# A graph network on one core: place registers loaded four at a time, restored columns queued behind x, widths built last, layer-one steps ahead of the drain

## What is computed

```python
h = relu(layernorm(x))
for W_r, W_sl, W_el in two_layers:
    agg = segment_sum((rel_embed[type] + h[src]) @ W_r, dst)
    h = rrelu(agg * deg ** -0.5 + where(deg == 0, h @ W_el, h @ W_sl))
x = x + h
h = relu(layernorm(x))
qk = h @ Wqk + bqk
scores = clip(sum(qk[dst] * qk[src]) / sqrt(128), -5, 5)
attn = segment_softmax(scores, dst)
x = x + layernorm(segment_sum(attn * v[src], dst) @ Wo + bo + h) * gamma + beta
```

## Time and profile before

| | before |
| --- | --- |
| median of 3 runs | 843.01 us (837.35 to 843.52) |
| the profiled execution | 839.33 us, span 836.7 us |
| mean granted TensorE clock | 0.973 |
| busy: PE, DVE, ACT, POOL | 722.0, 516.0, 431.7, 248.3 us |
| bytes moved by DMA | 27.89 MB, mean 33 GB/s |

### The profile page before, as it was taken

The page is one execution under the profiler, slowest core; times in us unless marked ns, Lnnn a source line. Parts: engine busy times, 40 slices in busy tenths (PEclk is TensorE's granted clock), DMA queues, the critical chain, the costliest instruction groups (busy, mean ns, idle before and its releaser), DMA issues.

```text
span 836.7 us, 15353 instructions
## 1 busy us (share of the span) xinstructions
PE 722.0 (86%) x5767; PEld 537.5 (64%) x5767; DVE 516.0 (62%) x931; ACT 431.7 (52%) x1085; POOL 248.3 (30%) x273
## 2 busy tenths in 40 slices
PE   4355787897879898988998899979999999999995
PEld 2245676797868788878887799834444444444455
DVE  4887997887767777724232333434475666565667
ACT  0435864555645555554211111257677676767672
POOL 7040020001001021110000000046666666666663
PEclk9999979999999999999999999999999999999997
DMA  4100200032310000010222211120000000000010
GB/s 127 41 1 16 60 5 8 2 94 75 98 46 8 8 8 7 7 63 3 66 65 87 63 38 38 38 97 15 1 13 12 13 13 11 15 3 23 1 26 18
DMA packets 39763, 27.89 MB, mean 33 GB/s; under 512 B 5311, under 2 KB 38163, under 8 KB 39686
## 3 DMA queue, kind: packets, MB, share of 16 engines
q1 hardware_dynamic: 38356, 26.02, 10.8%
q10 hardware_dynamic: 1330, 0.86, 0.4%
HBM read 13.28 MB, written 10.80 MB: 29 GB/s over the span
## 4 chain that ended last, share of the span: by engine, by line
PE 60%; DMA 10%; DVE 9%; issue 8%; ACT 7%; SPq 3%; ACTq 2%; POOL 1%; POOLq 0%; DVEq 0%
PE sums L1465 15%; PE sums L1448 15%; PE sums L997 9%; PE sums L1070 6%; PE sums L1036 6%; DMA work<-in_x 4%; DMA first_columns<-counts 2%; ACT counts L1238 2%; DMA h_attention<-work 2%; SPq L572 2%; DVE work L834 2%; DVE work L828 2%; ACTq L1214 1%; PE sums L1017 1%; PE sums L1004 1%
## 5 line engine op out<-in xcount | busy, mean ns | idle before, releaser
L1544 POOL TENSOR_TENSOR counts<-counts,work 125x500 f32<-125x500 f32 x150 | 165.5, 1104 | 96.6 <-DVE work L1605 89.5
L1036 PE MATMUL sums<-work 125*128 125x196 f16 (+15 forms) x1220 | 155.6, 255 | 24.6 <-DVE work L834 24.5
L1605 DVE SCALAR_TENSOR_TENSOR work<-sums,counts 125x500 f32<-125x500 f32 x150 | 101.7, 678 | 108.0 <-ACT sums L1562 108.0
L1465 PE MATMUL sums<-work 125*128 125x500 f32 (+1 forms) x350 | 158.6, 543 | 8.0 <-DVE work L1609 3.3
L828 DVE TENSOR_TENSOR work<-work,counts 125x3024 f16<-125x3024 f16 (+1 forms) x60 | 114.3, 1906 | 62.4 <-PE sums L1038 59.2
L1448 PE MATMUL sums<-work 128*125 128x500 f32 x300 | 150.3, 583 | 0.6 <-ACT work L1299 0.6
L1557 ACT ACTIVATE sums<-sums,work 125x500 f32<-125x500 f32 (+1 forms) x157 | 102.1, 650 | 76.3 <-PE sums L1448 73.0
L1238 ACT CAST counts<-sums 128x364 f32 (+38 forms) x305 | 132.1, 473 | 2.1 <-issue 1.4
L1038 PE MATMUL sums<-work 125*128 125x10 f16 (+15 forms) x800 | 132.5, 195 | 0.0
L997 PE MATMUL sums<-counts 125*128 125x250 f16 (+1 forms) x975 | 119.6, 267 | 9.5 <-ACT work L1180 9.5
L834 DVE TENSOR_TENSOR work<-work,counts 125x4200 f16<-125x4200 f16 (+15 forms) x120 | 125.5, 1087 | 0.0
(11 more groups left out here) (177 smaller groups left out, 660.9 us busy)
## 6 DMA issues: line engine op xcount, KB each, us to landing
first_columns<-counts SPq DMA_DIRECT2D x5, 610.4 KB
counts<-first_columns SPq DMA_DIRECT2D x5, 610.4 KB
counts<-counts SPq DMA_DIRECT2D x5, 468.8 KB
counts<-in_x SPq DMA_DIRECT2D x5, 312.5 KB
h_nodes<-counts SPq DMA_DIRECT2D x5, 312.5 KB
work<-in_x SPq DMA_DIRECT2D x12, 125.0 KB
x_after_messages<-work SPq DMA_DIRECT2D x12, 125.0 KB
h_attention<-work SPq DMA_DIRECT2D x12, 125.0 KB
```

Of the source, the lines that this page charges most:

```text
L1036: pe.matmul(win[:, 0:c, cols], lo[:, k * 2 * LO:k * 2 * LO + 128], m[:, k, h0 * w:(h0 + c) * w].rearrange("p (h d) -> p h d", d=w), start= ...
L1465: last = pe.matmul(ps_o[c % 2][:, 0:cols(u) // n], h3[:, j + i, :], pbuf[u % PB][:, i * NP:i * NP + cols(u) // n], start=j + i == 0, stop= ...
L1544: pool.tensor_tensor(a, a, p, ALU.add).then_inc(acc_done, 1)
L1605: dve.scalar_tensor_tensor(pbuf[u % PB], ps_s[u % 4][0:NP, 0:WIDE], float(np.exp(-CLIP)), counts[0:NP, j, c * WIDE:(c + 1) * WIDE], ALU.ma ...
```

## The change

Four edits. ScalarE loads the place registers four at a time (`CHUNK = 4`), so 50 loads of 4 take the place of 10 loads of 20. SyncE queues the restore of the columns directly behind the x load of its chunk instead of behind the h3 store. GpSimd builds `w_c` behind the identity matrix and signals `tables_done` a first time before it (with the memset of `power`) and a second time after it (with the memset of `one`), and VectorE waits for the second ahead of the first use of `w_c`. ScalarE's own, self and rest steps stand between the carry copy and the drain of their group.

```diff
@@ -607,13 +607,13 @@
                     sp.wait_ge(L["h3_out"], 16 * i)
                     sp.wait_ge(L["h3_turned"], i)
                 sp.dma_start(xc, by_block(x, c)).then_inc(L["x_in"], 16)
+                if i < 5:
+                    v = slice(5 * i, 5 * i + 5)
+                    sp.dma_start(counts[0:NP, v, 0:HEAD], heads.rearrange("p (j d) -> p j d", d=HEAD)[:, v, :]).then_inc(heads_in, 16)
                 sp.wait_ge(L["x2_ready"], i + 1)
                 sp.dma_start(by_block(x2, c), tmp).then_inc(L["x2_out"], 16)
                 sp.wait_ge(L["h3_ready"], i + 1)
                 sp.dma_start(h3[:, c * LB * D:(c + 1) * LB * D], xc.rearrange("p b f -> p (b f)")).then_inc(L["h3_out"], 16)
-                if i < 5:
-                    v = slice(5 * i, 5 * i + 5)
-                    sp.dma_start(counts[0:NP, v, 0:HEAD], heads.rearrange("p (j d) -> p j d", d=HEAD)[:, v, :]).then_inc(heads_in, 16)
             sp.wait_ge(L["summed"], CHUNKS)
             sp.wait_ge(L["h3_out"], 16 * LAST)
             for i, (j0, j1) in enumerate(T["h3_pieces"]):
@@ -651,18 +651,18 @@
             link(pool.tensor_scalar(starts, starts, 0.0, None, ALU.max))
             by_group(limit, [(0, float(KEY_AT - SPANS[1])), (KEY_GROUP, float(PART_AT - SPANS[1])), (PART_GROUP, float(N + PAD - SPANS[1]))])
             by_group(room, [(0, float(SPANS[0] - 1)), (ONE_BANK, float(SPANS[1] - 1))])
-            widths = [(first_group(b), float(w)) for b, (_, w) in enumerate(BATCHES) if b == 0 or w != BATCHES[b - 1][1]]
-            by_group(w_c, widths)
             pool.memset(power, -0.5).then_inc(tables_done, 1)
-            pool.iota(iota_f, pattern=[[1, NB * WM + WM % 2]], base=0, channel_multiplier=0).then_inc(iota_done, 1)
             pool.memset(ident_h[:, :], 0.0).then_inc(consts, 1)
             pool.wait_ge(consts, 1)
             pool.affine_select(out=ident_h[:, :], in_=ident_h[:, :], compare_op=ALU.not_equal, fill=1.0, base=0,
                                pattern=[[-1, 128]], channel_multiplier=1).then_inc(consts, 1)
+            widths = [(first_group(b), float(w)) for b, (_, w) in enumerate(BATCHES) if b == 0 or w != BATCHES[b - 1][1]]
+            by_group(w_c, widths)
+            pool.memset(one, 1.0).then_inc(tables_done, 1)
+            pool.iota(iota_f, pattern=[[1, NB * WM + WM % 2]], base=0, channel_multiplier=0).then_inc(iota_done, 1)
             by_group(least, [(0, 0.0)] + [(READY[c], float(LB * NP * (c + 1))) for c in range(CHUNKS - 1)])
             pool.memset(carry[:, 0, :], 0.0).then_inc(carry_ready, 1)
             pool.memset(ones_h, 1.0).then_inc(outside_set, 1)
-            pool.memset(one, 1.0).then_inc(outside_set, 1)
             pool.memset(T["outside"][:, :], 0.0).then_inc(outside_set, 1)
             pool.wait_ge(tables_done, 1)
             pool.wait_ge(stats_done, NB)
@@ -726,6 +726,7 @@
             link(dve.tensor_scalar(t_f, src_i, float(-(NP // 2)), 1.0 / NP, ALU.add, ALU.mult))
             link(dve.tensor_scalar(hi, t_f, ROUND, -ROUND, ALU.add, ALU.add))
             dve.scalar_tensor_tensor(key16[0], hi, float(-NP), src_i, ALU.mult, ALU.add).then_inc(nat_done, 1)
+            dve.wait_ge(tables_done, 2)
             for h in range(2):
                 last = dve.scalar_tensor_tensor(halves(key16[1], h), halves(hi, h), w_c[:, h:h + 1], halves(loc, h), ALU.mult, ALU.add)
             last.then_inc(nat_done, 1)
@@ -755,7 +756,7 @@
                 link(dve.tensor_tensor(by_tile(bad[:, 2:2 + RT]), by_tile(nx), over(w_c), ALU.is_ge))
                 link(dve.tensor_tensor(bad[:, 2 + RT:2 + 2 * RT], base, tb, ALU.is_lt))
                 link(dve.tensor_tensor(bad[:, at + 1:at + 3], by_tile(base)[:, :, 0], limit, ALU.is_gt))
-                dve.wait_ge(outside_set, 3)
+                dve.wait_ge(outside_set, 2)
                 link(dve.tensor_tensor(bad[:, at + 3:at + 5], by_tile(base)[:, :, 0], least, ALU.is_lt))
                 link(dve.memset(bad[:, at + 5:], 0.0))
                 link(dve.tensor_scalar(bad[0:1, at + 5:], base[0:1, 0:1], 0.0, None, ALU.is_gt))
@@ -974,7 +975,7 @@
                     if c:
                         pe.wait_ge(agg_out, c if c <= DIRECT else DIRECT + 1 if c == LAST else DIRECT)
                     else:
-                        pe.wait_ge(outside_set, 3)
+                        pe.wait_ge(outside_set, 2)
                         pe.wait_ge(flagged, 1)
                         pe.wait_ge(rest1[1], 1)
                     if c == HEAD_CHUNK:
@@ -1207,7 +1208,7 @@
                 act.copy(parts_t[:, v, s, :], xs[:, v, :]).then_inc(rounded1[s], 1)
 
             act.wait_ge(words_in, 16)
-            CHUNK = 20
+            CHUNK = 4
             for g in range(GROUPS):
                 if g % CHUNK == 0:
                     regs = [act.alloc_register(f"place{g + k}") for k in range(CHUNK)]
@@ -1231,6 +1232,10 @@
                     else:
                         act.copy(slot.rearrange("p (b h) -> p b h", b=2)[:, :, :, None],
                                  buf[:, :, 0:14 * span].rearrange("p b (h d) -> p b h d", d=span)[:, :, :, bass.ds(step, 1)]).then_inc(carry_ready, 1)
+
+                for kind, q, _ in slots[g]:
+                    if kind in ("own", "self", "rest"):
+                        layer1(kind, q)
                 c = reach(g)
                 if g:
                     act.wait_ge(put, 2 * g)
@@ -1245,9 +1250,6 @@
                 for s in range(2):
                     if g in ROUNDS[s]:
                         round1(ROUNDS[s].index(g), s)
-                for kind, q, _ in slots[g]:
-                    if kind in ("own", "self", "rest"):
-                        layer1(kind, q)
 
             def split(i, s):
                 v = slice(*PIECES2[i])
```

## The result

The change takes 805.41 us, the median of 4 runs (803.2 to 807.83), against 841.1 us for the kernel before in the same measurement. The ratio is 0.958, with a 95% interval of 0.9527 to 0.9633. The prediction said 803 us (792 to 818).

The account below looks back on a forecast made before the run. VectorE was taken to bound to 127 us, VectorE and TensorE to 168.4, SyncE's queue to 240.8, then TensorE, with transfers in layer two's early chunks. 2.5+7.8+6.5+1.8+10.0+10.5-1.2 = 37.9 us off 839.3 gave 801.4, taken as 803 (792 to 818).

Parts of the forecast that it names:

- the terms of the table: Forecast gains between seven successive marks, first one-hot batch to end of span: 2.5, 14.3, 1.8, 10.0, -1.2, 10.5, 0 us.
- Register loads: ScalarE's loads of four take 0.93 us, nearly covered; gains 7.8 us up to 127 us, 1.5 from 241 us.
- The term of the next stretch: 127 to 168.4 us: fewer stops from two loads and two chunks' layer-one waits, gain 6.5 us, bounds 4 and 8.2.
- some 35 us must remain: 127 to 168.4 us: the least time left, given VectorE's 32.2 us of work and TensorE's 33.4.
- Steps ahead of the drain: From 241 us: ScalarE's steps come 0.74 us earlier, gaining 4.4 and 5.1 us on two waits, less 1.0.
- The queue: 168.4 to 240.8 us: SyncE's transfers bind, gain only 1.8 us; ScalarE waits about 4 us at chunks 3 and 4.
- Widths last: Kernel start: line 714 starts 2.8 us earlier, `w_c` is 0.6 us late; gain 2.5 us, bounds -2.3 and 2.8.
- no full stop: GpSimd's chain of fifteen: beside VectorE's wide operations a step slows to 0.80 us instead of being locked out.
- Columns behind x: Layer two: five x loads freed from the restore, gain 10.5 us, bounds 5 and 11.7; weights delayed, -1.2 us.
- shared alike, the last weights come 1 to 2 us later: Layer two's start: first restore competes with ScalarE's six weight loads, -1.2 us, bounds 0 and -3.5.
- The loads are dearer: Rival, chance 0.14: all 50 loads cost 380 ns a register, 1.43 us for four; about 815 us.
- The other three rivals: Queue doesn't bind, 796 us (0.10); layer two stays transfer-bound, 812 (0.11); slower or level, loads mostly fixed-price (0.07).

Follow-up runs that it names:

- change_again: The change itself measured once more, against the kernel before: 804.75 us, ratio 0.9588.
- stores: The change with `store(2)` issued behind the writes of the first columns and `store(3)` ahead of the moved parts: 798.46 us, ratio 0.9501 to the kernel before.
- restore1: The change with its five restores one chunk later, behind x of layer two's second to sixth chunk: 800.14 us, ratio 0.9511 to the kernel before.
- u_restore: The change with the restore of the columns behind the h3 store again: 811.31 us, ratio 0.9644 to the kernel before.
- both: The change with `store(2)` and `store(3)` earlier and eight restores behind x of layer two's second to ninth chunk: 794.91 us, ratio 0.9475 to the kernel before.

## Why the prediction came out

**The sum.** 37.9 us were forecast and 36.1 measured between the two profiled executions. The mechanisms were right, and that the sum is so close is partly luck: the terms of the table missed by -0.1, +2.3, -1.1, -1.3, -1.7, +0.6 and -0.5 us. Undoing the parts one by one costs 16, 11, 5.4 and 3.6 us by the ratios, together 36, so no large overlap shows. Each of these is the difference of two ratios with intervals of some 0.005 to either side, 4 us, so a small one could not be seen.

**Register loads: right, and the largest part.** The price of the median load was right to 0.02 us. The sum of 46 us for 50 loads was not: it is 60, since 13 of them ran longer. That 0.93 us is covered and only 4.3 is not was too simple as well: with two registers a load the same kernel is another 5.9 us faster. In the stretch of the earlier trace rows, up to the batch behind group 80, the gain was 8.1 for 7.8. The term of the next stretch, was too small: 6.5 forecast with an upper bound of 8.2, 8.5 measured. The step that failed is "some 35 us must remain". I took TensorE's 33.4 busy us as they stood, though the clock of that stretch was 0.91. After the change it is 1.00 there, TensorE's work takes 31.1 us, and 32.8 us remain, 31.8 of them VectorE's. So here the stops gave back their own length and 2.3 us of work at the lower clock. Such a gain exists only where TensorE counts: in change_again the clock was 0.58 from 44 to 116.5 us, where VectorE sets the pace, and `store(1)` still falls at 149.36.

**Steps ahead of the drain: right.** 4.2 us and 3.2 us of the two waits went from 241 us on (4.4 and 5.1 forecast), and undoing the edit costs 11 us. That term was a little too high: 2.4 us of the wait at 998 stay, likely because a load or a drain can still stand ahead of the own steps; no run separates this.

**The queue: right.** It was the forecast that the middle stretch would hardly shrink, and that ScalarE would wait for `h_layer_one`. The stretch gave 0.7 us for 1.8; of the two waits one is 5.18 us (3.7 in change_again) for about 4, the other 1.10 instead of 4. TensorE was late itself there: behind ScalarE's first wait it stood still for 5.6 us, then ran at a clock of 0.88 up to chunk 4's self (0.97 before; busy 22.5 us instead of 20.2), and it waited another 1.5 us for carries behind the loads at 200.0 and 208.7, which took 4.5 and 2.8 us. "stores" shows that the limit was real.

**Widths last: right.** 2.4 for 2.5. GpSimd's chain took 7.42 us, VectorE's first use of `w_c` waited 0.90 us (0.6 forecast):

```profile
5.90 7.42 POOL L641 TENSOR_SCALAR_AFFINE_SELECT counts<-counts 100x2 f32<-100x2 f32 x15
...
7.31 0.16 DVE L714 TENSOR_TENSOR counts<-counts 100x2 f32<-100x2 f32 x1
...
13.51 1.39 DVE L731 SCALAR_TENSOR_TENSOR counts<-counts 100x500 f16<-100x500 f32 x2 [0.90 <-POOL counts L661]
```

I had read the 0.80 us a step as a mere slowing, "no full stop". The single steps show otherwise (the change, 8.7 to 13 us):

```profile
8.75 1.19 DVE L723 TENSOR_TENSOR counts<-counts 100x1000 f16<-100x1000 int32 x1
8.88 1.11 POOL L641 TENSOR_SCALAR_AFFINE_SELECT counts<-counts 100x2 f32<-100x2 f32 x1
...
11.41 1.20 DVE L728 SCALAR_TENSOR_TENSOR counts<-counts 100x1000 f16<-100x1000 f32 x1
11.57 1.09 POOL L641 TENSOR_SCALAR_AFFINE_SELECT counts<-counts 100x2 f32<-100x2 f32 x1
...
12.80 0.19 POOL L641 TENSOR_SCALAR_AFFINE_SELECT counts<-counts 100x2 f32<-100x2 f32 x1
```

An affine select of GpSimd that starts during a VectorE operation of 1000 columns ends 0.04 to 0.05 us after that operation, in all four cases (lines 723, 726, 727 and 728), though two of these last 0.68 us and two 1.2; alone it takes 0.19 us. The Trainium skill's rule of a full lock (page "SBUF — State Buffer", section "SBUF: two separate sides") agrees with this. What was wrong was what I made of it: I let all the last steps wait until VectorE waits, 1.8 us, while one step gets done with each VectorE operation. So four steps were slow and not five or six, and the wait was 0.90 us.

**Columns behind x: right in the loops (11.1 for 10.5), off at the weights.** -2.9 instead of -1.2. The failed step is "shared alike, the last weights come 1 to 2 us later": they came 3.7 us later, past the 3 us that the prediction itself named as a sign of being wrong, though the term stayed inside its bound of -3.5. This load was the last of five weight loads on ScalarE's queue, and those ahead of it were held up too (`Wqk` landed after 4.3 us instead of 2.0). restore1 and u_restore show that the restore is the cause; whether the half kilobyte waited behind the restore or behind its own queue isn't separated.

**The rivals.** "The loads are dearer" had the wrong form. It priced a slow load per register (380 ns, 1.43 us for four). Of the 50 loads 37 took 0.9 to 1.0 us, eleven 1.1 to 2.8, and two over 4. The floor of 600 ns that the Trainium skill's page "DMA: Bandwidth & Descriptors" gives in "Latency and other measured facts" isn't borne out here: one register took 286 ns, two took 488. The other three rivals did not come: the middle stretch shrank by 0.7 us and not by 5 to 6, the five loops take 11.1 us each, and the median load takes 0.91 us, below the 1.5 from which the change would have been slower.

## What to carry to other kernels

An in-order engine that others wait for should not stop for longer than the buffers behind it cover: here loads of 4 registers beat loads of 10 and of 20, and loads of 2 beat those of 4, though all loads together took longer (51 us by twenties, 62 by tens, 60 by fours, 68 by twos). Between 20 and 10 the intervals overlap. Before counting a gain, look for a queue that runs through the stretch untouched: it takes whatever the engines save, and its order is the next thing to change. A large transfer put behind a small one frees that one, and holds up the small ones issued after it, here even those on another engine's queue.

## What the runs showed of the hardware

A register load on ScalarE costs 0.29 us and 0.20 to 0.21 us for each further register: 286 ns for one, 488 for two, 912 for four, 2176 for ten, 4346 for twenty (medians). A load that runs while SyncE's large transfers between SBUF and DRAM or within SBUF are under way can take up to 8 us more. The longest were 7.5 us for twenty, 10.5 for ten, 5.6 for four ("both") and 3.6 for two, beside the moved parts; beside the writes of `h_nodes` (70 to 95 us in the change) loads of four took up to 2.4 us and those of twenty 6.5. Other loads beside the same transfers took their usual time. What decides it wasn't tried and stays open.
